# An encoder-decoder of 3x3 convolutions on one core: 32-row products in the two up stages, and four reorderings around them

## The reference

```python
def basic_block(x, w1, w2, stride=1, ds=None):
    out = relu(conv3(x, w1, stride) * BN_S)
    out = conv3(out, w2, 1) * BN_S
    identity = conv1x1(x, ds, stride) * BN_S if ds is not None else x
    return relu(out + identity)

def net(x):
    x = basic_block(x, e0b0c1, e0b0c2)
    x = basic_block(x, e0b1c1, e0b1c2);                       f0 = x
    x = basic_block(x, e1b0c1, e1b0c2, stride=2, ds=e1b0ds)
    x = basic_block(x, e1b1c1, e1b1c2);                       f1 = x
    x = basic_block(x, e2b0c1, e2b0c2, stride=2, ds=e2b0ds)
    x = basic_block(x, e2b1c1, e2b1c2)
    x = (relu(deconv2(x, dec0w) * BN_S) + f1) * BN_S
    return (relu(deconv2(x, dec1w) * BN_S) + f0) * BN_S

out = x + net(group_norm(x))
```

## Time and profile before

| | us |
|---|---|
| median of 3 runs (94.33 to 94.56) | 94.34 |
| the profiled execution | 94.52 |
| its span, first to last instruction | 92.5 |
| PE busy | 87.0 (94%) |
| PE weight loads busy | 77.4 (84%) |
| DVE busy | 66.2 (72%) |
| ACT busy | 42.9 (46%) |
| POOL busy | 26.4 (28%) |

### The profile page before, as it was taken

One profiled execution on the slowest core, in us unless ns is written; L12 is line 12 of the kernel. 1 busy time (PEld: TensorE's weight loads), 2 busy tenths in 40 slices (PEclk: granted clock), 3 DMA queues, 4 the chain that ended last, 5 costly groups with the idle time before them and its releaser, 6 DMA issues.

```text
span 92.5 us, 1508 instructions
## 1 busy us (share of the span) xinstructions
PE 87.0 (94%) x517; PEld 77.4 (84%) x517; DVE 66.2 (72%) x185; ACT 42.9 (46%) x88; POOL 26.4 (28%) x44
## 2 busy tenths in 40 slices
PE   5999999999999999999999999999999999999920
PEld 3678899997777799999877779989899999878920
DVE  5569979679998997466524679999766896246860
ACT  6007014076846663455403399899000599930100
POOL 7400061558770003433420003008830025000300
PEclk9999999999999999999999999999999999999999
DMA  1889800004358133710000000000000000000084
GB/s 30 255 248 353 254 22 4 7 0 101 98 175 283 51 113 113 172 62 0 0 0 0 0 4 0 0 0 0 7 0 0 0 4 0 7 0 0 19 299 136
DMA packets 4184, 6.51 MB, mean 70 GB/s; under 512 B 465, under 2 KB 2001, under 8 KB 4177
## 3 DMA queue, kind: packets, MB, share of 16 engines
q1 hardware_dynamic: 4176, 6.42, 22.5%
HBM read 5.37 MB, written 1.05 MB: 69 GB/s over the span
## 4 chain that ended last, share of the span: by engine, by line
PE 77%; DVE 14%; ACT 3%; issue 2%; DVEq 0%
PE psum L787 65%; PE psum L814 8%; DVE split L739 3%; DVE shared L729 2%; ACT split L533 2%; DVE block L707 2%; ACT shared L509 1%; PE psum L901 1%; DVE shared L674 1%; DVE result L777 1%; DVE shared L658 1%; DVE shared L701 1%; DVE shared L667 1%; DVE relu L701 1%; PE psum L965 1%
## 5 line engine op out<-in xcount | busy, mean ns | idle before, releaser
L465 POOL TENSOR_TENSOR odd<-relu,odd 128x363 fp32r<-128x363 f32 x12 | 12.1, 1009 | 17.4 <-ACT odd L537 17.4
L787 PE MATMUL psum<-shared,w_e0b0c 128*128 128x364 f32 x72 | 12.7, 332 | 0.1
L787 PEld LDWEIGHTS psum<-shared,w_e0b0c 128*128 128x128 f32 x72 | 11.9, 188 | 0.6 <-DVE shared L630 0.3
L787 PE MATMUL psum<-shared,w_e0b1c 128*128 128x364 f32 x72 | 12.2, 329 | 0.0
L787 PEld LDWEIGHTS psum<-shared,w_e0b1c 128*128 128x128 f32 x72 | 12.1, 188 | 0.1
L701 DVE SCALAR_TENSOR_TENSOR relu<-psum,inside 128x363 f32<-128x363 f32 (+2 forms) x18 | 8.8, 491 | 4.6 <-PE psum L787 4.6
L787 PE MATMUL psum<-odd,w_e0b0c 128*128 128x512 f32 x48 | 11.9, 410 | 0.0
L787 PE MATMUL psum<-odd,w_e0b1c 128*128 128x512 f32 x48 | 11.9, 410 | 0.0
L537 ACT ACTIVATE odd<-relu 128x363 fp32r<-128x363 f32 x12 | 6.2, 519 | 11.0 <-DVE relu L701 11.0
L787 PEld LDWEIGHTS psum<-odd,w_e0b0c 128*128 128x128 f32 x48 | 9.1, 190 | 2.5
L787 PEld LDWEIGHTS psum<-odd,w_e0b1c 128*128 128x128 f32 x48 | 9.1, 190 | 2.5
(11 more groups left out here) (127 smaller groups left out, 146.8 us busy)
## 6 DMA issues: line engine op xcount, KB each, us to landing
out<-result SPq DMA_DIRECT2D x3, 256.0 KB, 2.6
x_sb<-x_in SPq DMA_DIRECT2D x4, 160.0 KB, 3.8
raw<-e0b0c_in SPq DMA_DIRECT2D x2, 256.0 KB, 4.8
raw<-e0b1c_in SPq DMA_DIRECT2D x2, 256.0 KB, 5.0
raw<-e1b1c_in SPq DMA_DIRECT2D x2, 256.0 KB, 2.6
raw<-e2b1c_in SPq DMA_DIRECT2D x2, 256.0 KB, 2.6
raw<-e1b0c_in SPq DMA_DIRECT2D x1, 448.0 KB, 3.9
raw<-e2b0c_in SPq DMA_DIRECT2D x1, 448.0 KB, 3.3
```

What stands on the lines that cost most here:

```text
L465: pool.tensor_tensor(split_of(piece, 1), fp32_of(piece), split_of(piece, 0).bitcast(F32), ALU.subtract).then_inc(lo_ready, 1)
L787: last = pe.matmul(target, w, moving, start=(first and n == 0), stop=(final and n == len(terms) - 1), skip_group_check=skip)
```

## The change

Four things are edited.

1. **Up stages.** The products of dec0 and dec1 take only the 32 rows of weights and map that are not zero: four products, one on each quadrant, make a "round", into four banks. dec0 is 12 products of 32 rows. In dec1 the skip f1 is no longer added by GpSimd and DVE: PE multiplies it by `w_dec1w` too (`skip_round`), so dec1 has, for each of the 2 rows, 3 rounds on the skip and 3 on relu(dec0): 48 products of 32 rows and 256 columns in place of 24 of 128 rows. Two of the skip rounds stand before e2b1c1, in place of the fillers. GpSimd now copies f1's hi and lo into order (4 copies of 256 elements, after a wait for DVE's corners) in place of 4 additions of 128. relu(dec0) is split by one ACT and one DVE operation for each row. The results come in two groups of four; 3 and 7 are made by ACT (relu) and GpSimd (addition), the others by DVE.
2. **Head.** The lo products of piece 0 are held until piece 2 as well. DVE does `add_stats(1)` before the normalised rows and lo of image 0. `masks([1, 2])` move behind the eighth piece.
3. **Additions of x.** GpSimd's first addition waits until the lo of image 1's e1b0c1 map is written (before: of image 0's).
4. **Sides of image 1.** ACT copies the first part of its two rows and of the last one early, the second part after the lo planes; DVE copies three second parts and that of the last row, no longer all of that row. `scale_skip0(0)` moves behind them.

```diff
@@ -459,23 +480,25 @@ GpSimd
+            wait_half(pool, last_piece(STAGE["e1b0c1"], range(IMAGES), 0), 1)
             for image in range(IMAGES):
-                wait_half(pool, last_piece(STAGE["e1b0c1"], [image], 0), 1)
                 pool.wait_ge(skip0_scaled, image + 1)
                 pool.tensor_tensor(normed[:, image], normed[:, image], x_sb[:, image], ALU.add).then_inc(skip0_added, 1)
...
-            pool.wait_ge(sides_by_dve, 2 * IMAGES)
-            for q in range(4):
...
-                last = pool.tensor_tensor(skip1[:, i, :, j], hi, lo, ALU.add)
-            last.then_inc(skip1_ready, 1)
...
-            up_lo(pool, DEC0[1], up_lo_second)
+            pool.wait_ge(corner_by_dve, 1)
+            for i in range(2):
+                for j in range(2):
+                    first = FRONT[1]
+                    source = even[1][:, :, :, first + i:first + BLOCKS[1]:2, first + j:first + BLOCKS[1]:2]
+                    last = pool.tensor_copy(skip1[:, :, i, j], source.bitcast(F32))
+                last.then_inc(skip1_ready, 1)
+
+            for count, n in enumerate(sorted(BY_ACT)):
+                pool.wait_ge(skip0_ready, IMAGES)
+                pool.wait_ge(result_relu, count + 1)
+                pool.tensor_tensor(result[:, n], result[:, n], skip0_of(n), ALU.add).then_inc(result_added, 1)
...
+            wait_half(act, LEVEL0[-2].index, 1)
+            for copy in SIDES[:SIDES_BY_ACT[1, 1]] + SIDES[-1:]:
+                act.activation(*side_copy(1, 1, copy, (0, EARLY_RUN)), ACT.Copy)
+            wait_half(act, LEVEL0[-1].index, 1)
+            for copy in SIDES[:SIDES_BY_ACT[1, 1]]:
+                last = act.activation(*side_copy(1, 1, copy, (EARLY_RUN, RUN_1)), ACT.Copy)
+            last.then_inc(sides_by_act, 1)
             scale_skip0(0)
-            gather_sides(1, 1)
             gather_corners(1, 1)
...
-            wait_relu(act, DEC0[1].index)
-            act.activation(split_of(DEC0[1], 0), fp32_of(DEC0[1]), ACT.Copy).then_inc(up_hi_second, 1)
+            for row in range(2):
+                act.wait_ge(dec0_summed, row + 1)
+                act.activation(up_half(0, row), dec0_sums(row), ACT.Relu).then_inc(up_hi, 1)
+            for n in sorted(BY_ACT):
+                act.wait_ge(last_summed, n // 4 + 1)
+                act.activation(result[:, n], last_bank(n), ACT.Relu).then_inc(result_relu, 1)
...
+            for row in range(2):
+                dve.wait_ge(up_hi, row + 1)
+                dve.scalar_tensor_tensor(out=up_half(1, row), in0=dec0_sums(row), scalar=0.0,
+                                         in1=up_half(0, row).bitcast(F32), op0=ALU.max,
+                                         op1=ALU.subtract).then_inc(up_lo, 1)
...
+            def dec1_round(row, part, moving, first=False, final=False):
+
+                w = w_sb[W_INDEX["dec1w"]]
+                for q in range(4):
+                    lines = slice(CH * q, CH * q + CH)
+                    last = pe.matmul(last_bank(4 * row + q), w[lines, part, q],
+                                     moving[lines, row].rearrange("p (j i n) -> p i j n", j=2, i=IMAGES),
+                                     start=first, stop=final, skip_group_check=True)
+                return last
...
+                if stage.name == "e2b1c1":
+                    wait_relu(pe, last_piece(STAGE["e1b1c2"], range(IMAGES), 0))
+                    pe.wait_ge(skip1_ready, 1)
+                    wait_w_lo(pe, W_INDEX["dec1w"])
+                    skip_round(0, 0)
+                    skip_round(0, 1)
...
+                if piece.index == 0:
+                    target_0, low_terms_0 = target, low_terms
+                    continue
...
+            wait_half(pe, DEC0[0].index - 1, 0)
+            dec0_round(range(3), 0, hi, first=True)
+            dec0_round(range(3), 1, hi)
+            wait_half(pe, DEC0[0].index - 1, 1)
+            dec0_round(range(0, 2), 0, lo, final=True).then_inc(dec0_summed, 1)
+            dec0_round(range(2, 3), 0, lo, final=True)
+            dec0_round(range(3, 4), 0, hi, first=True)
+            dec0_round(range(3, 4), 1, hi)
+            dec0_round(range(3, 4), 0, lo, final=True).then_inc(dec0_summed, 1)
+
+
+            skip_round(0, 2)
+            pe.wait_ge(up_hi, 1)
+            dec1_round(0, 0, up[:, 0])
+            dec1_round(0, 1, up[:, 0])
+            pe.wait_ge(up_lo, 1)
+            dec1_round(0, 0, up[:, 1], final=True).then_inc(last_summed, 1)
+            pe.wait_ge(up_lo, 2)
+            pe.wait_ge(skip1_ready, 2)
+            for n in range(3):
+                skip_round(1, n)
+            pe.wait_ge(up_hi, 2)
+            dec1_round(1, 0, up[:, 0])
+            dec1_round(1, 1, up[:, 0])
+            dec1_round(1, 0, up[:, 1], final=True).then_inc(last_summed, 1)
```

More of the change, by code:

```diff
@@ L61 @@
 FILL = 2
[L62 to L65 removed]
+DEC0_BANKS = [4, 5, 6, 7]
+BY_ACT = {3, 7}
 RAW_SLOTS = 4
@@ L356, in split_of, with dec0_sums, up_half, last_bank @@
             return even_inside(stage.level, half, piece.images, piece.row, piece.rows)
[L358 to L363, removed]
+        def dec0_sums(row):
+            return psum[:, DEC0_BANKS[2 * row]:DEC0_BANKS[2 * row] + 2, 0:128]
+        def up_half(half, row):
+            return up[:, half, row].rearrange("p (j n) -> p j n", j=2)
+        def last_bank(n):
+            return psum[:, n, 0:256]
+        def skip0_of(n):
+            return skip0[:, n].rearrange("p i j a b -> p (i j a b)")
         def side_copy(level, image, copy, run=(0, RUN_1)):
@@ L425, in _ @@
             for first, count in stores:
-                sp.wait_ge(result_ready, first + count)
+                done = range(first + count)
+                sp.wait_ge(result_ready, len([n for n in done if n not in BY_ACT]))
+                if any(n in BY_ACT for n in done):
+                    sp.wait_ge(result_added, len([n for n in done if n in BY_ACT]))
                 sp.dma_start(out[:, first:first + count], result[:, first:first + count]).then_inc(stored, 16)
@@ L626, in norm, with norm_lo_rows @@
                                       ALU.subtract).then_inc(w_lo_first, 1)
+            def norm_lo_rows(image):
+                row, rows = NORM_ROWS[0]
                 norm_rows(image, 0)
@@ L665, in side_starts @@
                 first = SIDES_BY_ACT[1, 1]
-                for copy in SIDES[first:first + EARLY_COPIES]:
+                for copy in SIDES[first:-1]:
                     dve.tensor_copy(*side_copy(1, 1, copy, (0, EARLY_RUN)))
@@ L671, in side_rests @@
                 first = SIDES_BY_ACT[1, 1]
-                for n, copy in enumerate(SIDES[first:]):
-                    run = (EARLY_RUN if n < EARLY_COPIES else 0, RUN_1)
-                    last = dve.tensor_copy(*side_copy(1, 1, copy, run))
+                for copy in SIDES[first:]:
+                    last = dve.tensor_copy(*side_copy(1, 1, copy, (EARLY_RUN, RUN_1)))
                 last.then_inc(sides_by_dve, 1)
@@ L713, in _ @@
                     weights_lo(piece.index)
+                if piece is LEVEL0[7]:
+                    masks([1, 2])
                 if piece is LEVEL0[-2]:
@@ L814, in warm_up, with skip_round @@
                     pe.matmul(psum[:, bank, 0:256], zeros[:, 0:P], zeros[:, 0:256], start=True, stop=True)
+            def dec1_round(row, part, moving, first=False, final=False):
[6 more added lines that the diff above has]
+                return last
+            skip_flat = skip1[:].rearrange("p h r j i a b -> p h r (j i a b)")
+            skip_rounds = [(0, 0), (1, 0), (0, 1)]
+            def skip_round(row, n):
+                part, half = skip_rounds[n]
+                dec1_round(row, part, skip_flat[:, half], first=(n == 0))
             pe.wait_ge(ground_set, 1)
@@ L978, in _, with dec0_round @@
-            w = w_sb[W_INDEX["dec1w"]]
-            wait_w_lo(pe, W_INDEX["dec1w"])
-            wait_relu(pe, LAST[0].index - BANKS)
-            warm_up(FILL, LAST[0].index % BANKS)
-            for n, half in LAST_ORDER:
-                piece = LAST[n]
-                source, q = up[:, half, piece.row // 4], piece.row % 4
-                wait_source(piece, half)
-                if half == 0:
-                    wait_relu(pe, piece.index - BANKS)
-                    products(bank_of(piece)[:, 0:256], [(w[:, part, q], source) for part in range(2)], final=False)
-                else:
-                    products(bank_of(piece)[:, 0:256], [(w[:, 0, q], source)], first=False).then_inc(summed, 1)
+            def dec0_round(quadrants, part, moving, first=False, final=False):
+                for q in quadrants:
+                    lines = slice(CH * q, CH * q + CH)
+                    last = pe.matmul(psum[:, DEC0_BANKS[q], 0:128], w[lines, part, q], moving[lines],
+                                     start=first, stop=final, skip_group_check=True)
+                return last
```

81 lines of the change are left out of this document (24 added, 57 removed).

## The result

The changed kernel takes 93.06 us (median of 4 runs, 92.89 to 93.48), the kernel before 94.45 (4 runs, 94.33 to 94.61): a ratio of 0.986, 95% interval 0.984 to 0.988. The forecast was 92.6, a ratio of 0.982. So it is faster, by some three quarters of what was forecast. The profiled execution is the slowest of the four, 93.48 us, and its span is 91.3.

A forecast was written before the change was run, and what follows sets the result against it. PE's stream was taken to set the time nearly everywhere. 94.52 - 0.19 - 0.19 - 0.20 + 0.10 - 1.30 = 92.74 us, with the median 0.18 lower: 92.6; own range 92.0 to 93.2, 8-in-10 range 91.8 to 95.3.

The forecast's parts named there:

- Head: Start of the kernel: holding piece 0's lo products removes PE's wait for DVE; gain 0.19 us (bounds 0 and 0.3).
- Sides: Side products of image 1: shorter ACT and DVE copies close PE's gap; gain 0.19 us, 0 if ACT copies cost 0.55.
- Additions of x: Level 1: with GpSimd's wait moved, its addition no longer stretches DVE's L729; gain 0.20 us (bounds -0.2 and 0.2).
- Level 2: GpSimd's four skip copies, 0.5 us each, run over DVE's lo operation; loss 0.1 us (bounds 0 and 0.45).
- rival D: Up stages: the array runs empty where products change from 128 to 32 rows and back; 92.8 us, chance 0.15.
- The round: Up stages: four 32-row products mostly overlap and cost 0.20 us together (from below 0.14, from above 0.57).
- Rival A: Up stages: a round's four weight loads stand in a line, 0.11 us apart, 0.43 a round; 95.5 us, chance 0.20.
- dec0 to the last store: Up stages: last store issued at 88.15 instead of 89.45; gain 1.3 us (1.65 with rounds of 0.14).
- The end: Behind the last DVE result: only the last store and its landing are left, 3.05 us that no edit touches.
- The sum: Whole kernel: gains 0.19, 0.19, 0.20 and 1.30, loss 0.10, from 94.52 to 92.74 us; median of runs 92.6.

The follow-up runs named there:

- e12: The changed kernel unaltered, run again as the measure for later store and weight-load variants: 93.01 us.
- e7: The changed kernel with GpSimd's first addition of x released by image 0's map, as in the kernel before: 93.16 us.
- e1: The changed kernel with all products of the up stages on 128 rows, the weights' other rows zero: 96.18 us, 1.0154 of the kernel before.
- e5: The changed kernel with the head as before (piece 0 not held, DVE's order and the masks as before): 93.76 us.
- e8: The changed kernel with three stores (4, 2 and 2 results) in place of five: 93.62 us.
- e9: The changed kernel with three stores (1, 3 and 4 results) in place of five: 92.61 us, 0.980 of the kernel before.

## Why the prediction was right or wrong

**Head, 0.19 forecast: 0.22.** Mechanism and size held. PE runs 16 products at a stretch with no wait for DVE where the earlier trace rows had one; the timeline of the changed kernel:

```profile
7.82 0.63 ACT L503 ACTIVATE w_e0b0c<-raw 128x512 fp32r<-128x512 f32 x1 [0.82 <-DMA raw<-e0b0c_in]
...
8.55 2.97 PE L804 MATMUL psum<-shared,w_e0b0c 128*128 128x364 f32 x16 [0.87 <-ACT w_e0b0c L503]
```

What the prediction did not have is the start itself. These weights were 0.8 us late for ACT in this execution and not at all in that of before; in the twelve profiles of the experiments the first product comes anywhere from 7.96 to 8.71. e12, the same program, had 7.96. It is not an effect of the change, but one of the same size as its smaller terms.

**Sides, 0.19: 0.13.** The copies cost what was taken (ACT 0.44 and 0.47 each; DVE 0.15 less in all). Some of PE's gap is left (0.20 between starts, against 0.14 in a dense run): PE's next product starts 0.16 behind DVE's end, and I had DVE ending earlier than PE would ask.

**Additions of x, 0.20: 0.31.** The cause was right, e7 shows it. The size was the gap between two starts, and that is not all that a wait costs. The timeline of the kernel before, PE in the first 0.1 us behind the wait:

```profile
65.51 0.53 PE L787 MATMUL psum<-shared,w_e1b0c 128*128 128x256 f32 x2
```

Two products end 0.53 after the first starts; with a passage of 0.29 the second starts 0.24 behind the first, not 0.14. The term should have been 0.20 + 0.10.

**Level 2, -0.10: 0.** GpSimd's copies took 0.40 each, not 0.50, and ended at 77.61; DVE's lo operation took 0.39 instead of 0.35, within the slack that was named:

```profile
76.00 1.61 POOL L489 CAST skip<-even 128x256 fp32r<-128x256 f32 x4 [7.36 <-DVE corner L779]
...
77.42 0.39 DVE L750 TENSOR_TENSOR odd<-relu,odd 128x180 fp32r<-128x180 f32 x1
...
78.68 0.51 PE L838 MATMUL psum<-skip,w_dec1w 32*128 32x256 f32 x8
...
79.14 1.59 PE L804 MATMUL psum<-even,w_e2b1c 128*128 128x180 f32 x12
```

The two early rounds fit in the wait. The first 32-row product starts 0.21 behind the last of 128 rows (78.47). e1 has the same products in the same order there, all on 128 rows; its timeline:

```profile
77.34 1.56 PE L804 MATMUL psum<-odd,w_e2b0c 128*128 128x128 f32 x12
78.74 1.16 PE L837 MATMUL psum<-skip,w_dec1w 128*128 128x256 f32 x8
```

In e1 the distance is 0.11 (the last of the twelve starts at 78.62, the first of the eight at 78.74), so the change from 128 to 32 rows costs 0.1: the cause of rival D is there. It costs nothing here, for PE waits for its next map anyway: the first product of e2b1c1 starts 0.67 behind the last one of e2b0c in the changed kernel (78.47 to 79.14) as in the one before (78.84 to 79.51). What the change back to 128 rows costs is hidden by that wait. The Trainium skill, "TensorEngine Tiling (Array Packing)", section "Key Properties", speaks of a drain on a change of mode; the 0.1 agrees.

**The round, 0.20: 0.11.** It lies below my lower bound of 0.14, and that bound was misread. I had taken it from the 3.42 us of dec1's 24 products, but five of their 23 distances, 0.18 to 0.23 long, are no dense run: PE waits there or has just waited. Where nothing is waited for, at the end of the kernel before, it is this:

```profile
88.03 0.52 PE L787 MATMUL psum<-shared,w_dec1w 128*128 128x256 f32 x3
```

With the passage of 0.28 taken off, the starts are 0.12 apart. So a full product costs 0.12, four of them 0.47 and not 0.57, and of the 0.03 that I called a product's own cost only 0.01 is one. A round costs no more than one full product: the 256 columns at 2.4 GHz are 0.107 of it, and the four share them. Rival A, loads in a line, fell: 0.02 apart, not 0.11. (By its own formula its early rounds would have been 2 x 0.43 - 0.55 = 0.31 late, not 0.35.) The 3.07 times of the Trainium skill ("TensorE: Matmul & The Clock Gate", section "Measured speedup vs the span model") was nearer than rival A, and still too careful for this stream: 0.46 / 0.11 is 4.2, though against full products in the same order.

**dec0 to the last store, 1.3: 1.43.** The timeline of the changed kernel, to be read against the earlier trace rows:

```profile
83.12 0.74 PE L1002 MATMUL psum<-even,w_dec0w 32*128 32x128 f32 x10 [0.15 <-DVE even L729]
...
83.89 0.66 ACT L582 ACTIVATE shared<-psum 128x256 fp32r<-128x256 f32 x2 [2.65 <-PE psum L1002]
...
84.31 0.76 DVE L785 SCALAR_TENSOR_TENSOR shared<-psum,shared 128x256 fp32r<-128x256 f32 x2 [0.85 <-ACT shared L582]
84.33 0.85 PE L838 MATMUL psum<-shared,w_dec1w 32*128 32x256 f32 x12
...
85.31 2.08 DVE L795 SCALAR_TENSOR_TENSOR result<-psum,skip 128x256 f32<-128x256 f32 x6 [0.24 <-PE psum L838]
...
85.76 2.31 SPq L432 DMA_DIRECT2D out<-result  x5
...
86.68 0.73 POOL L495 TENSOR_TENSOR result<-result,skip 128x256 f32<-128x256 f32 x1 [0.18 <-ACT result L585]
...
87.17 0.90 SPq L432 DMA_DIRECT2D out<-result  x2
```

Row 0 is summed 0.77 after dec0's start (forecast 0.72), the last store is issued at 87.66, 4.54 after it (forecast 4.67); before it was 89.45 - 83.48 = 5.97, so 1.43 is gained. That this is so near the forecast is in part luck, for two errors cancel. With rounds of 0.11 row 1 is summed 3.03 after dec0 (86.15), and the forecast had 3.45. But then 1.51 pass to the last store, where it had 1.22. DVE is still busy with row 0: it works on the six results without a pause and ends at 87.39, together with GpSimd (87.41), and not earlier. And SP issues the last store 0.25 behind them, because its issue before, begun at 87.17, has to end first (the last row above holds both). The forecast had no such wait.

**The end, "3.05 us to the span's end, which no edit touches": this is the step that failed.** It is 91.3 - 87.66 = 3.64 in the changed kernel, 0.59 more, and what took its place is a queue of stores. The stores' 5.54 us from the first issue on are nearly those of before, so the gain from dec0 on is that of the first store, 0.75, plus 0.09, and not the 1.43 of the last. 0.59 of what was saved up to the last store went into that queue. I had looked at the last store alone, and not at the share of the 16 engines behind the first one. It was high already in the kernel before, in these stretches (columns as above):

```profile
88.00:89.00 1.00, 0.55 (x5) 0.34 (x3) 1.00 (x3) 0.00 (x0) 0.00 (x0) 1.00 0.82 286
89.00:90.00 1.00, 0.00 (x0) 0.00 (x0) 0.42 (x2) 0.00 (x0) 0.00 (x0) 1.00 0.78 295
90.00:91.00 1.00, 0.00 (x0) 0.00 (x0) 0.00 (x0) 0.00 (x0) 0.00 (x0) 1.00 1.01 344
```

At shares of 0.8 and 1.0 there was little idle time to take out, so a last store issued 1.43 sooner could not end 1.43 sooner: the bytes ahead of it were still under way. e5 bears this out: its last store is 0.49 later than the changed kernel's, its end 0.07.

**The sum.** 0.22 + 0.13 + 0.31 + 0 + 0.84 = 1.50 against a forecast of 1.78. The end alone took 0.59 from the forecast; the other terms together came out 0.31 better than forecast and hid half of that. The measured medians are 1.39 apart.

## What to carry to other kernels

When a stage ahead of the output gets faster, ask what flows out. While the stores follow each other closely, the end is set by the volume from the first store on: an earlier first store counts, fewer and larger stores count, and an earlier last store does not. Products whose weights are zero outside 32 rows are worth cutting even at twice their number, if, as here, the four quadrants follow each other into four banks (fewer banks were not tried). To read what a product costs, take a run of products without a wait in it, not a total over many. And judge edits of 0.1 to 0.3 us by distances between marks in the trace: they repeat to 0.05 us where the times of whole runs do not.

## What the runs showed of the hardware

- **The clock falls near the end, at a moment that varies.** With the new up stages TensorE's granted clock drops from 2.4 to 1.2 GHz in e5 at about 84.8 us and in e8 at about 84.4, in the middle of the rounds, in the changed kernel at about 86.3, behind them. In the profiled execution of the kernel before it stayed up to the end; in e1, with full rows, it was still up at 93.0. e5's stretches (columns as above) and its twelve skip products:

```profile
84.50:85.00 0.50, 0.50 (x12) 0.32 (x8) 0.50 (x2) 0.00 (x0) 0.00 (x0) 0.80 0.00 0
85.00:86.00 1.00, 1.00 (x20) 0.95 (x20) 0.62 (x2) 0.38 (x1) 0.16 (x1) 0.50 0.00 0
```

```profile
85.05 1.01 PE L833 MATMUL psum<-skip,w_dec1w 32*128 32x256 f32 x12
```

1.01 us instead of 0.63. It delayed e5's last store by 0.49 us, but its end by 0.07 only. In e8 it makes up some 0.2 of the 1.0 us by which the first store is later: in e9 the same four results can be stored 3.45 after dec0, in e8 3.67. What keeps the clock up was not tried.
- **Four products of 32 rows run side by side.** A round costs 0.11 us where the same four on 128 rows cost 0.46, and the change from 128 to 32 rows costs 0.1 more.
- **The first product behind a wait is followed late.** The second one starts 0.24 us behind the first in the kernel before (65.51), where a dense run of the same products has 0.13.
- **Fewer and larger stores.** Stores of 1, 3 and 4 results moved the same 1.05 MB in 4.84 us from the first issue to the end, five of 1 and 2 in 5.57.
